# A fused vision block on one core: stages moved between steps, two sets of DMAs given to ScalarE's queue

## The chip, the cores and the metric

One core of a Trainium2 chip runs one launch of the kernel. The metric is device time in microseconds (us). Engines are named as in the profile: PE is TensorE (PEld its weight loads), DVE is VectorE, ACT is ScalarE, POOL is GpSimd, SP is the sync engine, which here only starts DMAs.

## The reference

Input x is 128 images of 12 x 224 x 224 in float32, 308 MB. Three stages follow each other; LN is a layer norm over the last axis.

```python
pooled = x.reshape(B, 12, 14, 16, 14, 16).sum(axis=(3, 5))        # 16x16 patch sums
h = einsum('bcij,ce->bije', pooled, channel_weights)              # (128, 196, 192)
y = LN(h); q = y[:, :64]; k = v = y[:, 64:]
a = softmax(einsum('bqc,bkc->bqk', q, k) / 4) @ v                 # 64 queries, 132 keys
a = transpose(a, (0, 2, 1)).reshape(B, 64, 192) @ proj_w.T + proj_b
h = h + concatenate([a, k], axis=1)
z = LN(h); scores = sigmoid(z @ gate_weight.T)                    # 8 experts
w, idx = best 2 of 8, limited to the best 2 of 4 pairs
out = h + sum over the 2 experts of w * ((silu(z@w1.T) * (z@w3.T)) @ w2.T) + the same for a shared expert
```

## The kernel before

**Groups and steps.** The images go in 8 groups of 16. The expert layers of a group are 63 steps: 7 chunks of rows times 9 experts (8 routed, the ninth shared). Chunks 0 to 4 (steps 0 to 44) are the key tokens, 384 to 512 rows each, whose first layer is one bf16 matmul per half (L1524). Chunks 5 and 6 (steps 45 to 62) are the queries, whose first layer is five fp32r matmuls per half (L1353). A step on each engine:

- PE, step s: first half of layer 1 for step s+1, second half for step s, layer 2 of step s-2 (L1509), then the items that a plan puts at step s. Before the first of these it waits for the silu of step s-1, whose PSUM bank it overwrites.
- ACT, step s: the silu of step s+1 (L913), at steps 1, 10, 19, ... an eviction of the chunk's output (L890), then its items, then its part of a tile of x (L801, one instruction per patch column).
- POOL, step s: multiplies silu by the gate weight row (L752), then items.
- DVE, step s: h = product of both halves (L1266), items, its part of a tile (L960).
- SP: one DMA per routed step that spreads one gate weight row over 128 partitions (L561, 5 steps ahead), the loads of x (1.8 MB a tile, 3 slots, L506), the stores, the stacking copies.

ACT loads a function table whenever it changes between silu and exp.

**Items.** While group g is in its expert layers, two plans bring the next data along. AK_PLAN (steps 39 on, group g+1): tok and V (patch sums transposed), stats and pow (variances, power on POOL), Xw and X (key rows in bf16 pieces), Uw and U, 28 gate operations of DVE (gate_k, L1177 to L1226), CK (gate weights to DRAM by ACT's queue). AQ_PLAN (steps 0 to 38, group g): PHT and VHT (transposed heads; VHw is their DVE part), S (scores), exp (L822), sum, ET (transposed probabilities, L1416), AH (times values, L1421), M (projection, L1426, copied to Msb by ACT L856), then H (L1449 and L1450: the residual rows, 8 rounds), stat_q, x2, XT (L1458), GQ, G, gate_q, CQ (L1482). Between M and H four DMAs (L532) of each half stack Msb into Mst; H waits for their semaphore `mixed`. MIX says that SP issues them at steps 11 and 17.

**Tiles.** 21 tiles of x per group: EARLY gives steps 1 to 34 to ten of them (three parts each, in three steps running), LATE steps 40 to 61 to eleven (two parts). A part costs DVE one reduce and ACT 1 to 3 columns. POOL takes two columns of each of the first 31 tiles (pool_tile, L663 and L658).

**Head.** Before group 0 there are no expert layers: 21 tiles are summed as they land, then steps 39 to 62 of the plans run alone for group 0, together with eleven tiles of group 1. Then the first silu starts. The groups 1 to 4 run in a hardware loop of two groups per turn.

## Time and profile before

| | us |
|---|---|
| median of 3 runs | 1794.09 |
| lowest and highest | 1784.72, 1795.03 |
| profiled execution, its own time | 1794.41 |
| its span in the profile | 1792.6 |
| head, until the first h | 198 |
| one group | 197 to 207 |
| PE busy | 1509.6 |
| DVE busy | 1178.3 |
| ACT busy | 879.1 |

Busy time is the sum of an engine's instructions; DMA-issuing instructions are not in it, although they hold the queue of the engine that issues them. In timeline rows the number in brackets is how long the engine had been idle before the row, with what released it.

### The profile page before, as it was taken

How to read it: one execution, taken by the hardware profiler on the slowest of the kernel's cores; microseconds unless marked ns; L12 is line 12 of the kernel's file. 1: busy time of each engine (PE TensorE's matmuls, PEld its weight loads, DVE VectorE, ACT ScalarE, POOL GpSimd, SP SyncE). 2: the span in 40 equal slices, each digit the busy share in tenths (PEclk: the TensorE clock that was granted, in tenths of full speed). 3: DMA queues.
4: the chain of work that ended last, by engine and by line, in shares of the span. 5: the costliest groups of instructions: out<-in, count | busy, mean ns of one | idle time of the engine just before them, and what ended most of it. 6: DMA issues, size and time to landing. Idle time of an engine off the chain costs nothing. (4 is left out here: it accounts for less than half of the span.)

```text
span 1792.6 us, 29976 instructions
## 1 busy us (share of the span) xinstructions
PE 1509.6 (84%) x9094; PEld 1184.0 (66%) x9094; DVE 1178.3 (66%) x2060; ACT 879.1 (49%) x2809; POOL 761.5 (42%) x761
## 2 busy tenths in 40 slices
PE   1721698999899988989899988999899988999997
PEld 1201575877668765877668765777668765887686
DVE  5856686687768666667768676677768666355511
ACT  2333655556545645547535655546545644335310
POOL 4327244633373234623464243633373233733431
PEclk9955799999999989999999999999999989999998
DMA  9897777778677777777777687768777775223320
GB/s 341 358 361 276 300 276 272 276 276 291 245 280 260 281 262 268 273 275 274 256 247 297 241 292 278 276 253 299 256 263 280 268 262 158 70 64 111 96 84 24
DMA packets 127672, 440.11 MB, mean 246 GB/s; under 512 B 14221, under 2 KB 80930, under 8 KB 105998
## 3 DMA queue, kind: packets, MB, share of 16 engines
q1 hardware_dynamic: 126390, 436.79, 67.6%
q10 hardware_dynamic: 1112, 1.30, 0.3%
q8 instruction: 76, 1.25, 0.3%
q14 instruction: 94, 0.77, 0.1%
...
## 5 line engine op out<-in xcount | busy, mean ns | idle before, releaser
L752 POOL TENSOR_TENSOR ffn<-ffn 128x384 f32<-128x384 f32 (+2 forms) x448 | 510.3, 1144 | 888.7 <-ACT ffn L913 810.2
L1509 PE MATMUL bank<-W2T,ffn 128*128 128x192 f32 (+1 forms) x3600 | 705.7, 333 | 10.2 <-ACT stage L890 5.0
L1509 PEld LDWEIGHTS bank<-W2T,ffn 128*128 128x128 f32 (+1 forms) x3600 | 604.9, 191 | 79.8 <-issue 16.5
L1266 DVE TENSOR_TENSOR ffn<-bank,ffn 128x384 f32<-128x384 f32 (+2 forms) x504 | 310.4, 617 | 349.3 <-PE bank L1353 151.8
L960 DVE TENSOR_REDUCE pooled<-xt 128x3 f32<-128x768 f32 (+2 forms) x375 | 447.8, 1195 | 18.5 <-DMA xt<-in_x 17.9
L913 ACT ACTIVATE ffn<-bank 128x384 f32<-128x384 f32 (+2 forms) x504 | 272.3, 542 | 370.3 <-PE bank L1524 141.3
L801 ACT ACTIVATE xt<-xt 128x256 f32<-128x256 f32 x809 | 329.7, 414 | 83.7 <-DMA xt<-in_x 76.1
L1524 PE MATMUL bank<-X2T,Wx 126*128 126x384 bf16 (+2 forms) x720 | 202.6, 355 | 46.7 <-DVE ffn L1266 31.9
L801 ACT ACTIVATION_READ_ACCUMULATOR xt<-xt 128x1 f32 x809 | 158.6, 196 | 0.0
L1353 PE MATMUL bank<-x0h,WT0h 128*128 128x512 f32 x288 | 130.5, 453 | 6.0 <-DVE ffn L1266 6.0
L1524 PEld LDWEIGHTS bank<-X2T,Wx 126*128 126x128 bf16 x720 | 58.2, 100 | 103.7 <-DVE ffn L1266 46.1
L1353 PE MATMUL bank<-x1l,WT1s 128*128 128x512 f32 x288 | 113.9, 395 | 0.0
L1353 PE MATMUL bank<-x1h,WT1s 128*128 128x512 f32 x288 | 113.8, 395 | 0.0
L1353 PE MATMUL bank<-x0l,WT0h 128*128 128x512 f32 x288 | 113.6, 395 | 0.0
L1353 PE MATMUL bank<-x0h,WT0l 128*128 128x512 f32 x288 | 113.6, 394 | 0.0
L707 POOL TENSOR_TENSOR stat<-stat,mhalf 98x16 f32<-98x16 f32 x32 | 94.8, 2970 | 21.9 <-DVE stat L1085 13.6
L1353 PEld LDWEIGHTS bank<-x0h,WT0h 128*128 128x128 f32 x288 | 54.3, 189 | 24.6 <-DVE ffn L1266 9.0
L1353 PEld LDWEIGHTS bank<-x1l,WT1s 128*128 128x128 f32 x288 | 54.0, 188 | 13.1
L1353 PEld LDWEIGHTS bank<-x0l,WT0h 128*128 128x128 f32 x288 | 54.0, 188 | 13.0
L1353 PEld LDWEIGHTS bank<-x1h,WT1s 128*128 128x128 f32 x288 | 54.0, 188 | 13.0
L1353 PEld LDWEIGHTS bank<-x0h,WT0l 128*128 128x128 f32 x288 | 54.4, 189 | 5.9
L841 ACT CAST UTq<-bank 126x128 bf16<-126x128 f32 x64 | 17.0, 265 | 84.0 <-PE bank L1433 84.0
...
## 6 DMA issues: line engine op xcount, KB each, us to landing
...
ffn<-cw_rows SPq DMA_DIRECT2D x192, 256.0 KB, 6.8
ffn<-cw_rows SPq DMA_DIRECT2D x192, 192.0 KB, 8.8
out<-stage SPq DMA_DIRECT2D x192, 96.0 KB
...
```

Of the source, the lines that this page charges most:

```text
L707: nc.gpsimd.tensor_tensor(out=stat[:, 3 * a + 1, u], in0=stat[:, 3 * a, u], in1=mhalf[0:HT, u], op=ALU.pow).then_inc(rstd_ready, 1)
L752: nc.gpsimd.tensor_tensor(out=cwb[slot][:, 0:n], in0=silu[(g.par + step) % 2][:, 0:n], in1=cwb[slot][:, 0:n], op=ALU.mult).then_inc(scaled, 1)
L801: last = nc.scalar.activation(src[:, :, j, :], src[:, :, j, :], ACT.Copy, accum_out=pooled[:, t // HALF, at:at + 1])
L841: nc.scalar.copy(UTq[:, :].rearrange("p (b t) -> p b t", b=GB)[:, 2 * i:2 * i + 2, :], src[:, :, 0:NQ])
L913: nc.scalar.activation(silu[(g.par + step) % 2][:, 0:n], h_ps(g, step, 0)[:, 0:n], ACT.Silu)\
L960: ins = v.tensor_reduce(out=pooled[:, t // HALF, at + lo:at + hi], in_=src[:, lo:hi, :, :], axis=AX.XY, op=ALU.add)
L1266: v.tensor_tensor(out=h[step % HR][:, 0:n], in0=h_ps(g, step, 1)[:, 0:n], in1=(silu[p] if e == NE else cwb[(c * NE + e) % CW_RING])[:, 0:n ...
L1353: ins = mm(o, left[q], right[q], start=(q == 0), stop=(q == len(left) - 1))
L1509: last = mm(o, h[step % HR][:, 128 * t:128 * t + m], W2T[:, e, :], start=(e == 0 and t % 2 == 0), stop=(e == NE), skip_group_check=True)
L1524: last = mm(o[:, 0:n], Wx[:, w:w + INTER], X2T[:, col:col + n], start=True, stop=True)
```

## The change

1. AQ_PLAN and AK_PLAN get other steps. PHT, VHT 0 and both VHw move from the group's start to the end of the group before (59 to 62); exp goes from steps 5 and 11 to 3 and 10, ET, S, M and H one step or so; gate_q is spread over steps 31 to 38 (3 or 4 a step) in place of 30 to 35 (5 a step); CQ goes from 36 to 39; the AK plan starts one step later and ends its gates two steps sooner, CK moves from 59 to 57, X takes three rounds a step.
2. EARLY becomes every third step from 1 to 28, LATE moves by a step or two.
3. The stacking copies ("mix") and the first five weight rows of a group ("row") are issued by ACT, at steps 11 and 18, and 60 and 61.
4. At every third step of a chunk (s % 9 == 2) PE does its items before layer 2.
5. In the head, POOL sums only group 0's tiles, and a table of its own (FIRST) says at which step DVE and ACT sum group 1's eleven.

```diff
 AQ_PLAN = {
...
-    5: [("U", 7), ("exp", 0)],
-    6: [("ET", 0), ("sum", 0)],
+    3: [("exp", 0), ("U", 7)],
+    4: [("sum", 0)],
+    5: [("ET", 0)],
...
-    11: [("exp", 1)],
+    10: [("exp", 1), ("M", 1)],
+    11: [("sum", 1), ("mix", 0)],
...
+    18: [("stat_q", 0), ("mix", 1)],
...
-MIX = {11: 0, 17: 1}
-A_FIRST = 39
+A_FIRST = 40
...
-    AQ_PLAN.setdefault(30 + _n // 5, []).append(("gate_q", _n))
-    AK_PLAN.setdefault(53 + _n // 5, []).append(("gate_k", _n))
+    AQ_PLAN.setdefault(31 + _n * 8 // GATES, []).append(("gate_q", _n))
+    AK_PLAN.setdefault(51 + _n // 5, []).append(("gate_k", _n))
...
-LATE = {s: i for i, s in enumerate([40, 44, 46, 48, 50, 52, 53, 55, 57, 59, 61])}
-EARLY = {s: len(LATE) + i for i, s in enumerate([1, 5, 8, 12, 16, 20, 23, 27, 31, 34])}
+LATE = {s: i for i, s in enumerate([41, 44, 46, 47, 49, 50, 52, 54, 56, 58, 60])}
+EARLY = {s: len(LATE) + i for i, s in enumerate([1, 4, 7, 10, 13, 16, 19, 22, 25, 28])}
+FIRST = {41: 0, 42: 1, 43: 2, 44: 3, 46: 4, 47: 5, 50: 6, 57: 7, 58: 8, 59: 9, 60: 10}
-POOL_TILES = TILES + len(LATE) - 1
+POOL_TILES = TILES
...
+                if kind == "mix":
+                    act.wait_ge(aux_act, g.at(BYACT[-1], BYACT[R[("M", 2 * i + 1)]]))
+                    for m in range(4):
+                        act.dma_start(Mst[:, 4 * i + m, :],
+                                      Msb[2 * CH * m:2 * CH * (m + 1), i, :]).then_inc(mixed[i], 16)
+                    return
+                if kind == "row":
...
+                    act.dma_start(cwb[i][:, 0:n], cw_rows[g.par, i, 1024:1024 + n].partition_broadcast(128))\
+                       .then_inc(cw_landed[i], 16)
...
                     layer1(g, step, 1)
+                    if step % EX == 2:
+                        step_pe(g, step, left)
                     if step >= 2:
                         layer2(g, step - 2)
...
-                    step_pe(g, step, left)
+                    if step % EX != 2:
+                        step_pe(g, step, left)
```

ACT's order around steps 10 to 13 of a group in the loop, before. L890 is the eviction, L856 the copy of M, L913 a silu, L822 the exp, L851 the copy of ET, L801 tile columns.

```order
L890 COPY stage<-bank 128x384 [waits out_stored1]
L890 COPY stage<-bank 128x192
L828 REGISTER_ALU
L856 COPY Msb<-bank 96x192 [waits aux_full]
L801 ACTIVATE xt,pooled<-xt 128x16x16 [waits x_in1]
...
L913 ACTIVATE ffn<-bank 128x384 [waits scaled]
L821 REGISTER_ALU
L822 ACT_TABLE_LOAD
L822 ACTIVATE attw<-attw 64x8x132 [waits aux_dve]
...
L913 ACT_TABLE_LOAD
L913 ACTIVATE ffn<-bank 128x384 [waits scaled]
```

The same place in the changed kernel, whose lines are 9 or 10 further on: L899 is the eviction, L812 the exp, L865 the copy of M, L791 tile columns, L922 a silu, L818 the stacking DMAs.

```order
L899 COPY stage<-bank 128x192
L811 REGISTER_ALU
L812 ACT_TABLE_LOAD
L812 ACTIVATE attw<-attw 64x8x132 [waits aux_dve]
...
L865 COPY Msb<-bank 96x192 [waits aux_full]
L791 ACTIVATE xt,pooled<-xt 128x16x16 [waits x_in2]
...
L922 ACT_TABLE_LOAD
L922 ACTIVATE ffn<-bank 128x384 [waits scaled]
...
L818 DMA h2q<-Msb 72x1x192 [waits aux_act]
L818 DMA h2q<-Msb 72x1x192 x3
...
L922 ACTIVATE ffn<-bank 128x384 [waits scaled]
```

Eviction and exp now stand between the same two silus, and the four DMAs stand ahead of the next one.

PE's order at step 20, before: the first H of the second half comes behind layer 2 (L1509).

```order
L1524 MATMUL bank<-X2T,Wx 128x512 [waits silu_done]
L1524 MATMUL bank<-X2T,Wx 128x512 [waits h_done]
L1493 REGISTER_ALU
L1509 MATMUL bank<-W2T,ffn 128x192 [waits evac_act]
...
L1449 MATMUL bank<-CWx,UTq 128x192 [waits mixed_second,aux_dve]
L1450 MATMUL bank<-h2q,CWr 128x192
```

In the changed kernel, where L1533 is layer 1, L1458 and L1459 are H, and L1518 is layer 2:

```order
L1533 MATMUL bank<-X2T,Wx 128x512 [waits silu_done]
L1533 MATMUL bank<-X2T,Wx 128x512 [waits h_done]
L267 REGISTER_ALU
L1458 MATMUL bank<-CWx,UTq 128x192 [waits mixed_second,aux_act]
L1459 MATMUL bank<-h2q,CWr 128x192
L1502 REGISTER_ALU
L1518 MATMUL bank<-W2T,ffn 128x192 [waits evac_act]
```

H, with its wait for the stacking DMAs, now stands ahead of layer 2.

## Rows read from the trace of the kernel before

**Rows 1.** The page: busy time, share of the span and instructions of each engine.

```profile
PE 1509.6 (84%) x9094; PEld 1184.0 (66%) x9094; DVE 1178.3 (66%) x2060; ACT 879.1 (49%) x2809; POOL 761.5 (42%) x761
```

**Rows 2.** Windows: head, group 1, last group. Length, then busy time of each engine.

```profile
0.00:198.00 198.00, 66.26 (x254) 31.82 (x254) 129.57 (x179) 69.03 (x303) 90.18 (x187) 0.73 0.86 328
396.60:595.00 198.40, 180.09 (x1118) 143.44 (x1118) 143.83 (x251) 110.28 (x359) 86.56 (x75) 0.99 0.76 275
1603.00:1792.00 189.00, 170.37 (x1036) 138.16 (x1034) 72.98 (x156) 58.62 (x113) 64.16 (x57) 0.98 0.27 79
```

**Rows 3.** Timeline of PE in group 1, rows that followed idle time.

```profile
397.88 0.68 PE L1402 MATMUL bank<-ident,attw 64*128 64x64 f32 x8 [1.87 <-DVE attw L1105]
411.70 0.62 PE L1416 MATMUL bank<-ident,attw 64*98 64x64 f32 x8 [1.84 <-issue]
428.34 0.62 PE L1416 MATMUL bank<-ident,attw 64*98 64x64 f32 x8 [0.92 <-issue]
437.74 0.26 PE L1449 MATMUL bank<-CWx,UTq 126*128 126x192 bf16 x1 [1.19 <-DMA h2q<-Msb]
451.56 0.63 PE L1458 MATMUL bank<-ident,attw 128*128 128x128 f32 x4 [1.09 <-DVE attw L1146]
480.35 0.50 PE L1524 MATMUL bank<-X2T,Wx 126*128 126x384 bf16 x2 [0.96 <-ACT ffn L913]
485.74 0.34 PE L1524 MATMUL bank<-X2T,Wx 126*128 126x384 bf16 x1 [2.08 <-DVE ffn L1266]
491.39 0.36 PE L1524 MATMUL bank<-X2T,Wx 126*128 126x448 bf16 x1 [0.83 <-DVE ffn L1266]
494.54 1.03 PE L1482 MATMUL bank<-ident,gt 128*8 128x128 f32 x8 [1.81 <-DVE gt L1226]
517.40 0.50 PE L1353 MATMUL bank<-x0h,WT0h 128*128 128x512 f32 x1 [0.78 <-DVE ffn L1266]
563.96 1.57 PE L1509 MATMUL bank<-W2T,ffn 128*128 128x192 f32 x8 [0.72 <-DVE stage L1247]
```

**Rows 4.** POOL's timeline: the first scaling of group 2 and the wait before it.

```profile
593.20 0.99 POOL L752 TENSOR_TENSOR ffn<-ffn 128x384 f32<-128x384 f32 x1 [8.86 <-DMA ffn<-cw_rows]
```

**Rows 5.** Window of DVE over the gate_q steps of group 1.

```profile
480.00:497.00 17.00, 14.82 (x36) 0.90 0.80 284
```

**Rows 6.** ACT's timeline, group 1, steps 10 to 12: eviction, M copy, table load, exp, tile column.

```profile
423.62 0.70 ACT L890 COPY stage<-bank 128x384 f32<-128x384 f32 x2 [0.17 <-PE bank L1509]
424.75 0.31 ACT L856 COPY Msb<-bank 96x192 f32<-96x192 f32 x1 [0.43 <-PE bank L1426]
...
425.86 1.28 ACT L822 ACT_TABLE_LOAD   x1
427.16 1.08 ACT L822 ACTIVATE attw<-attw 64x1056 f32<-64x1056 f32 x1
...
430.40 0.43 ACT L801 ACTIVATE xt<-xt 128x256 f32<-128x256 f32 x1
```

**Rows 7.** Windows over all engines from that eviction to step 14; one step with H.

```profile
423.62:430.88 7.26, 6.34 (x50) 5.06 (x49) 4.93 (x7) 6.77 (x14) 2.75 (x3) 1.00 1.01 408
442.32:444.17 1.85, 1.85 (x13) 1.57 (x12) 1.85 (x5) 1.25 (x5) 1.54 (x2) 1.00 0.87 340
```

**Rows 8.** DMA issues: four stacking copies on SP (timeline); setup copies on ACT (ns min/median/max).

```profile
426.64 3.40 SPq L532 DMA_DIRECT2D h2q<-Msb  x4
L816 ACTq DMA_DIRECT2D Wx<-ffn x6: 726/736/1339, 89.0 to 93.5; - x6
```

**Rows 9.** Group 2: PE's timeline at the first H, and the window after it.

```profile
638.16 0.34 PE L1449 MATMUL bank<-CWx,UTq 126*128 126x192 bf16 x1 [4.06 <-DMA h2q<-Msb]
640.00:650.00 10.00, 10.00 (x41) 7.72 (x40) 5.23 (x12) 4.22 (x15) 2.58 (x3) 0.65 0.57 199
```

**Rows 10.** Timeline of the head: POOL, DVE and ACT.

```profile
136.91 0.73 POOL L663 TENSOR_TENSOR ffn<-xt 128x256 f32<-128x256 f32 x1
138.86 2.91 POOL L707 TENSOR_TENSOR stat<-stat,mhalf 98x16 f32<-98x16 f32 x1
...
169.20 2.27 DVE L960 TENSOR_REDUCE pooled<-xt 128x8 f32<-128x2048 f32 x1
...
187.14 0.34 ACTq L872 DMA_DIRECT2D cw_rows<-attw  x1
...
195.84 0.87 ACT L913 ACTIVATE ffn<-bank 128x384 f32<-128x384 f32 x2
```

More of the change, by code:

```diff
@@ L107 @@
     27: [("XT", 3)],
[L108 to L113 removed]
+    29: [("GQ", 0), ("GQ", 1)],
+    30: [("G", 0)],
+    39: [("CQ", 0), ("CQ", 1)],
+}
+A_FIRST = 40
 AK_PLAN = {
[L115 to L135 removed]
+    40: [("fin", 0), ("tok", 0), ("V", 0)],
+    41: [("stats", 0), ("pow", 0)],
+    42: [("pow", 1)],
+    43: [("stats2", 0), ("pow", 2)],
+    44: [("pow", 3)],
+    45: [("Xw", 0)],
+    46: [("Xw", 1), ("Xw", 2)],
+    47: [("Xw", 3)],
+    48: [("X", 0), ("X", 1), ("X", 2)],
+    49: [("X", 3), ("X", 4), ("X", 5), ("Uw", 0)],
+    50: [("keyG", 0), ("keyG", 1), ("GK", 0), ("Uw", 1)],
+    51: [("Uw", 2)],
+    52: [("Uw", 3)],
+    53: [("U", 0)],
+    54: [("U", 1)],
+    55: [("U", 2)],
+    56: [("U", 3)],
+    57: [("CK", 0), ("CK", 1), ("CK", 2)],
+    58: [("CK", 3), ("CK", 4)],
+    59: [("PHT", 0)],
+    60: [("PHT", 1), ("VHw", 0), ("row", 0), ("row", 1), ("row", 2)],
+    61: [("VHT", 0), ("row", 3), ("row", 4)],
+    62: [("VHw", 1)],
 }
@@ L191, in tiles_at @@
         found.append((g.plus(1), EARLY[step]))
-    if left >= 2 and step in LATE:
-        found.append((g.plus(2), LATE[step]))
+    late = FIRST if g.k is None and g.off < 0 else LATE
+    if left >= 2 and step in late:
+        found.append((g.plus(2), late[step]))
     return found
@@ L550, in cw_load @@
                 back = use - CW_RING
-                if use == 0:
+                if use == CW_AHEAD:
                     sp.wait_ge(cw_out[0], g.at(16, 16))
@@ L564, in step_dma @@
             def step_dma(g, step, left):
-                if step >= 61 and left:
-                    for ahead in ((0, 1) if step == 61 else (2, 3, 4)):
-                        cw_load(g.plus(1), ahead)
-                elif step + CW_AHEAD < STEPS and g.off >= 0:
+                if step + CW_AHEAD < STEPS and g.off >= 0:
                     cw_load(g, step + CW_AHEAD)
@@ L588, in ffn_dma @@
                         store(g.minus(1), NCH - 1)
-                    if step in MIX:
-                        stack_mix(g, MIX[step])
             for t in range(TILES):
@@ L822, in item @@
                     nc.scalar.activation(E[:, :, NQ:TOK], E[:, :, NQ:TOK], ACT.Exp).then_inc(exp_done, 1)
+                    return
[4 more added lines that the diff above has]
+                                      Msb[2 * CH * m:2 * CH * (m + 1), i, :]).then_inc(mixed[i], 16)
+                    return
+                if kind == "row":
+                    if i == 0:
+                        act.wait_ge(cw_out[0], g.at(16, 16))
+                    back = i + CW_USES - CW_RING
+                    wait(act, h_done, g.minus(1).at(STEPS, back // NE * EX + back % NE + 1) if g.k is not None or g.off else 0)
+                    if i == CW_RING - 1 or g.k is None and g.off == 0:
+                        act.wait_ge(rows_used, POOL_TILES)
+                    n = CHUNKS[0][2]
+                    act.dma_start(cwb[i][:, 0:n], cw_rows[g.par, i, 1024:1024 + n].partition_broadcast(128))\
+                       .then_inc(cw_landed[i], 16)
                     return
```

58 lines of the change are left out of this document (13 added, 45 removed).

## The prediction

> **What bounds the kernel now.** I read the page's busy times first, then windows by group, then PE's timeline for the rows that follow idle time, then the engine each of them names. The page [rows 1] gives PE 84% of the span, DVE 66%, ACT 49% and POOL 42%: the bound is PE, but not at every place. The windows [rows 2] say where it isn't. In the head PE works 66.3 of 198 us. In group 1 it works 180.1 of 198.4 us, so 18.3 us of a group are idle, and in the last group 18.6 of 189.0. No other engine is near full in group 1 (DVE 143.8, ACT 110.3, POOL 86.6), so the 18.3 us are waits at single places, and only those can be won. PE's timeline [rows 3] has most of them: 1.87 at the group's start, 1.84 before ET of the first half, 0.92 before ET of the second, 1.19 at the first H, 1.09 at XT, 0.96 + 2.08 + 0.83 + 1.81 = 5.68 in the gate zone, 0.78 and 0.72 late in the group, together 14.1. A change that moves items can win those and can open new ones, since the items are a chain and the silus stand in the same ACT queue.
>
> **The change part by part.** All terms are for group 1 and taken for groups 0 to 6; the head and the last group follow. PE's arithmetic is the same in both kernels.
>
> Start of a group. PE waits 1.87 for VHT [rows 3], because POOL's scaling stood for 8.86 us until its first weight rows had landed [rows 4], behind x loads on SP's queue. Now ACT issues these rows at steps 60 and 61 and VHT is made a step before the border. The wait goes, and what is late next (the silu of step 1) has a step of PE work as cover: -1.9.
>
> ET of the first half. Two steps between exp and ET where there was one. The exp itself is two table loads of 1.28 and 1.08 of work [rows 6], which still stand between two silus, so the 1.84 shrinks to some 1.2: -0.6.
>
> Steps 10 to 14. This is the costliest edit. Before, the eviction stood at step 10 and the exp at 11. Now both stand between the silus of steps 11 and 12, with M's copy and two tile columns: 0.70 + 1.28 + 1.08 + 0.31 + 2 x 0.43, a load back 1.28 and the silu 0.44 (half of 0.87, [rows 10]) = 5.95 [rows 6]. PE can't start step 13 before that silu. Then come the four DMAs. Six setup copies on ACT's queue took a median of 736 ns each [rows 8], so 2.9 us; SP's four took 3.4. With two columns and the next silu that is 2.9 + 0.86 + 0.44 = 4.2 more, 10.2 in all. PE has 6.34 us of work in that window [rows 7], and 0.65 of it (scores, moved to step 9) is gone: 5.7. So 4.5 us of stall, 2.1 before step 13 and 2.4 before step 14, in place of 0.92 + 1.19 = 2.11 [rows 3] of which the second comes again as follows. H waits for the copies' landing. On SP the issue ended at 430.04 [rows 8] and H began at 437.74 [rows 3], 7.7 us later; I take 4.5 on ACT's queue, an estimate between that and nothing, which makes H some 1.9 late after the steps between. The bounds: from 0 (if the issue returns early, or falls where ACT waits for PE) to 5.1 (if landing takes 7.7 again). Sum 4.5 + 1.9 - 2.11, plus 0.4 for the shorter lead at ET: +4.7, bounds -2 to +8.
>
> Second half, steps 18 to 20. The DMAs are issued at 18, a step later than before, and H at 20 stands ahead of layer 2. From M on PE: copy 0.31, columns 0.86, silu 0.44, issue 2.9, landing 4.5 less what the first of four gains, about 3: 7.5. PE has two steps of 1.85 [rows 7] and an H round of 0.5, some 4.2, in that time: 3.3 of stall. XT's 1.09 [rows 3] behind it is absorbed: +2.2, bounds -1.1 (all covered) to +5.5.
>
> Gate zone. DVE is busy 14.82 of 17.00 us there [rows 5], so each wait of PE for h is a wait for a full DVE. Tile parts leave steps 31 to 38 (EARLY ends at 28) and the gates fall from five a step to three or four. The waits for DVE, 2.08 + 0.83 + 1.81 [rows 3], fall to about 1; the 0.96 behind ACT stays: -3.7, with bounds 0 and -5.7. The tile parts pushed forward meet a DVE that is busy 4.93 of 7.26 and 1.85 of 1.85 us [rows 7], so some of this comes back; I take 0.1.
>
> Late steps. 0.78 and 0.72 [rows 3] fall to 0.6 together by PE's order at every third step of a chunk and by CK two steps sooner, and X with three rounds a step on two PSUM banks costs 0.6: -0.3, bounds -1.5 to +1.
>
> A group: -1.9 - 0.6 + 4.7 + 2.2 - 3.6 - 0.3 = +0.5, and of that 0.2 is taken off because part of ACT's stall hides PE's waits for h in the same steps: +0.3, seven groups +2.
>
> Head. POOL's sum stood ahead of pow: 136.91 to 138.86 [rows 10], 2.0 us, and three such leave the chain that ends the head: -6. Behind it DVE did tile sums of 2.27 [rows 10] between gates, three of them in the chain: -6.8. But not all of the 12.8 is won, since ACT's tail is now the longer: CK's copies and DMAs from 187.14 [rows 10], tiles of four or five columns at 0.43 [rows 6], five rows at 0.74 [rows 8], the copies for PHT and a table load before the silu at 195.84 [rows 10]. By these some 3 us are won, and 1.7 us of group 0's first PE work is done in the head: -4.7. Bounds: 0 (ACT eats all) and -12.8. The head's loads of x (DMA share 0.86, [rows 2]) don't change.
>
> Last group. No tiles and no next group: 4.7 and 2.2 without the columns' shares (3.9 and 1.5), start and ET -2.5, gates -1: +2.
>
> Clock. After a wait of 4.06 us at an H in group 2, the granted clock over the next 10 us was 0.65 of full [rows 9], partly the lower level of 1.2 GHz instead of 2.4. Stalls of 2 and more at steps 13, 14 and 20 could bring that; shorter waits in the gate zone could save some. I set 0, bounds -12 (1.7 a group saved) and +28 (3.5 a group: at 0.65 ten microseconds hold 6.5 of work).
>
> The sum: 1794.4 of the profiled execution (span 1792.6 and 1.8 around it) + 2 - 4.7 + 2 = 1793.7. That execution lay 0.3 above the median of 1794.1, so the forecast is 1793.4, rounded to 1793.5: the kernel gives back at steps 10 to 20 what it wins elsewhere.
>
> **Rivals.**
>
> R1, the issue on ACT costs PE nothing (faster). ACT has 88 us idle in group 1 [rows 2] and in parts of this zone waits for PE; if exp and DMAs fall into those, or if the four copies land soon after issue, then the +4.7 and +2.2 shrink to 0 or below. Seven a group over 7.5 groups is 52: 1741; with half of it 1767. For it speaks the 7.7 us that SP's copies took to land in one place [rows 8] and the 4.06 wait in the next group [rows 9]: SP's queue is the one with the x loads, and a queue of its own may have them land in 2. Against it speaks ACT's 6.77 busy of 7.26 us in just this window [rows 7], before anything was added. The Trainium skill bears on this: DMA: Bandwidth & Descriptors, Queues, rings and completion order, says that each DMA engine takes turns between the queue rows it has work for, packet by packet, and SP and ACT have a row each. By this rule ACT's copies don't wait behind a whole x load and R1's landing holds. No run here yet shows it.
>
> R2, slower: the stall before H starves PE long enough for the clock. Its place is steps 13 to 15 and 20. If landing on ACT's queue takes the 7.7 us of SP's [rows 3, 8], H is 3.2 later; if after it the clock does what [rows 9] show, 3.5 go with it. One of both in each group is 3.4 x 8 = 27: 1820; both are 54: 1847. It decides from a granted clock under 0.9 behind step 14 in most groups. For it: PE in this zone goes from 6.34 of 7.26 us to 5.7 of 10.2. Against: the gaps are short single ones, of 2 to 3 us, where the one shown was 4.06. The Trainium skill's own page, Trainium Kernel Development and Optimization, Key Constraints, says that queues of SP, ACT and POOL run on the same 16 DMA engines and that issuing from several saves only the issuer's time. By that, landing stays at 7.7 and this rival is the nearer one; the DMA share of 1.01 in [rows 7] agrees that the engines are full there.
>
> R3, the change doesn't do what it says. LATE now puts x tiles at steps 46 and 47 and at 49 and 50, one step apart, with three slots; a load can start only when the slot's last sum is done. If the second of each pair waits for its load, DVE and with it h is 1 to 3 us late twice a group, which takes back the gate zone's gain: 1794 + 7.5 x 3 = 1816 at worst.
>
> **How the numbers follow.** A measurement of this kernel can tell about 1% (18 us) from no change. The forecast, gains and losses within 18 us of each other: 0.42. R1, 0.34, centred on 1760 with a tail to 1735. R2 and R3 together 0.24 (0.18 and 0.06), centred on 1825. Range: below 1745 lies a quarter of R1, 0.08; above 1830 two fifths of the slower cases, 0.1. So 1745 to 1830; the likeliest case's own range is 1776 to 1812. Chances: faster by over 1% 0.34, within 1% 0.42, slower by over 1% 0.24.
>
> **What would show it.** POOL's wait at a group's start and PE's at VHT gone. ACT's timeline: the four DMAs of about 0.74 each between two silus, and PE idle 2 us before each of steps 13 and 14: if that idle is under 1, R1 is right. The first H's releaser: DMA with more than 2 us of idle is my forecast or R2, and a landing under 2 us after the issue is R1. PE's waits for h in the gate zone under 1.5 us together. The clock in the windows behind step 14 under 0.9: R2. First silu of the head near 193; if it is before 188, ACT's tail was costed too high. PE's idle in group 1 near 18.6 of about 198.7 us. A group under 194 or over 201 us would make the forecast wrong.

## The result, and the profile after

The changed kernel takes 1887.97 us (median of 4 runs, 1882.68 to 1891.90), the kernel before 1794.56 in the runs beside it: the ratio is 1.053, with a 95% interval of 1.047 to 1.058. The forecast was 1793.5 with a range to 1830. The change costs 93 us, and the forecast was wrong in sign and outside its range.

The page of the changed kernel, engine busy times, as in [rows 1]:

```profile
PE 1568.7 (83%) x9094; PEld 1233.2 (65%) x9094; DVE 1185.5 (63%) x2060; ACT 884.7 (47%) x2829; POOL 745.2 (39%) x721
```

PE executes the same 9094 matmuls and is busy 59.1 us longer. The span grew by 97.5 (1890.1 for 1792.6), so 59 of them are matmuls that ran at a lower clock, and 38 are idle time.

Windows of the changed kernel over the head, group 1 and the last group, columns as in [rows 2]; a group is cut at the end of its first h:

```profile
0.00:194.20 194.20, 70.73 (x278) 35.16 (x278) 132.50 (x183) 74.39 (x327) 71.82 (x146) 0.71 0.87 335
402.00:614.50 212.50, 187.26 (x1119) 149.89 (x1118) 143.80 (x251) 110.76 (x358) 86.99 (x75) 0.94 0.72 256
1697.90:1889.50 191.60, 170.72 (x1021) 138.28 (x1019) 72.36 (x153) 56.75 (x110) 64.08 (x57) 0.97 0.28 78
```

Group 1 is 212.5 long instead of 198.4: PE's busy time rose by 7.2 and its idle time from 18.3 to 25.2, while DVE, ACT and POOL work the same time as before. The granted clock over the group is 0.94 for 0.99.

Where in the group? Windows of PE by stage in group 1 of the kernel before, cut where DVE ends the h of a step. Shown are steps 15 to 17, 18 to 22, 31 to 40 and 48 to 50. After the PE busy time stand granted clock, DMA share and GB/s.

```profile
...
433.52:442.67 9.15, 7.96 (x53) 1.00 1.04 353
442.67:455.98 13.31, 12.01 (x72) 1.00 0.84 294
...
478.38:505.67 27.29, 20.21 (x103) 0.94 0.84 289
...
528.45:539.78 11.33, 11.31 (x65) 1.00 0.95 368
...
```

The same four stages in the changed kernel:

```profile
...
441.88:458.89 17.01, 10.82 (x71) 0.80 0.76 276
458.89:476.87 17.98, 14.07 (x69) 0.81 0.68 250
...
498.35:518.69 20.34, 17.46 (x106) 1.00 0.70 242
...
545.00:563.51 18.51, 13.70 (x76) 0.82 0.60 220
...
```

Steps 15 to 22 went from 22.5 to 35.0, and 48 to 50 from 11.3 to 18.5, each with a clock of 0.80 to 0.82 where it had been full. The gate zone fell from 27.3 to 20.3. With a whole group cut into four zones in the same way, the mean length over groups 0 to 6 is, before and after: steps 0 to 11, 30.7 and 33.2; 12 to 22, 31.4 and 44.0; 23 to 47, 72.7 and 67.6; 48 to the next 0, 65.9 and 70.0. So +2.6 + 12.6 - 5.1 + 4.0 = +14.1 a group, 99 for seven. The head is 3.8 shorter, the last group 2.5 longer, which makes the 97.5.

PE's timeline in group 1 of the changed kernel, rows after idle time, to be read against [rows 3] (L1458 is H, L1416 S, L1452 X, L1491 CQ):

```profile
407.78 0.30 PE L1416 MATMUL bank<-PHT,VHT 128*64 128x34 f32 x2 [1.05 <-DVE attw L1125]
409.90 0.43 PE L1442 MATMUL bank<-identb,SPT 98*126 98x98 bf16 x4 [0.70 <-DVE attw L1125]
417.29 0.50 PE L1533 MATMUL bank<-X2T,Wx 126*128 126x384 bf16 x2 [1.21 <-ACT ffn L922]
436.73 0.50 PE L1533 MATMUL bank<-X2T,Wx 126*128 126x384 bf16 x2 [2.14 <-ACT ffn L922]
448.06 0.34 PE L1458 MATMUL bank<-CWx,UTq 126*128 126x192 bf16 x1 [6.28 <-DMA h2q<-Msb]
466.81 0.32 PE L1458 MATMUL bank<-CWx,UTq 126*128 126x192 bf16 x1 [3.91 <-DMA h2q<-Msb]
...
506.06 0.34 PE L1533 MATMUL bank<-X2T,Wx 126*128 126x384 bf16 x1 [0.71 <-DVE ffn L1275]
508.40 0.36 PE L1533 MATMUL bank<-X2T,Wx 126*128 126x448 bf16 x1 [0.83 <-DVE ffn L1275]
516.62 1.03 PE L1491 MATMUL bank<-ident,gt 128*8 128x128 f32 x8 [0.90 <-DVE gt L1235]
...
551.06 2.17 PE L1452 MATMUL bank<-identb,SPT 98*126 98x34 bf16 x16 [4.51 <-DVE SPT L1073]
```

Three waits carry most of the idle time that was added: 6.28 before the first H (7.12 to 8.88 in groups 2 to 6), 3.91 before the fifth (1.5 in four of the six groups 1 to 6), and 4.51 before X, where before had none. The waits of the gate zone, 5.7 in sum before, are 0.71 + 0.83 + 0.90 now.

**What an idle PE costs afterwards.** Windows of PE in group 2, around the wait of 7.12 that ended at 661.3:

```profile
650.00:654.00 4.00, 3.34 (x24) 1.00 0.98 375
...
658.00:662.00 4.00, 0.71 (x3) 0.50 1.02 393
662.00:666.00 4.00, 4.00 (x21) 0.50 0.85 321
666.00:670.00 4.00, 4.00 (x29) 0.50 0.12 40
670.00:674.00 4.00, 4.00 (x12) 0.50 0.53 170
```

The clock is at its lower level of 1.2 GHz (0.50) before the wait ends, and stays there for 12 us of full work behind it. Steps 15 to 17 on PE, from the first matmul of one step's layer 1 to that of another, took 8.4 us before (the median of groups 1 to 5) and take 15.7 (10.2 and 10.4 in groups 1 and 4, 15.8 or 15.9 in 2, 3 and 5). At X it is the same on a smaller scale: 0.50 from 551 to 555, then 0.68.

In group 1 the clock had fallen already before the first H, behind the 2.14 us for ACT's silu:

```profile
437.00:441.00 4.00, 4.00 (x22) 0.64 0.99 370
```

Summed over the profile, the time at the lower clock in the four zones was 1.5, 3.4, 3.4 and 0.7 us a group before, and is 5.2, 18.5, 0 and 7.2 in the changed kernel.

### The profile page after: what moved, and what is told of

Same layout as the page of the kernel before. It is cut to its first block and busy times, and to the rows that moved or that the text cites. A ratio compares the mean times of both kernels' runs of the same rounds, so it can differ in the third digit from the quotient of the medians.

```text
span 1890.1 us, 29906 instructions
## 1 busy us (share of the span) xinstructions
PE 1568.7 (83%) x9094; PEld 1233.2 (65%) x9094; DVE 1185.5 (63%) x2060; ACT 884.7 (47%) x2829; POOL 745.2 (39%) x721
## 5 line engine op out<-in xcount | busy, mean ns | idle before, releaser
L742 POOL TENSOR_TENSOR ffn<-ffn 128x384 f32<-128x384 f32 (+2 forms) x448 | 512.0, 1147 | 1009.1 <-ACT ffn L922 964.8
L1518 PE MATMUL bank<-W2T,ffn 128*128 128x192 f32 (+1 forms) x3600 | 725.1, 340 | 3.6 <-DVE stage L1256 1.9
L1518 PEld LDWEIGHTS bank<-W2T,ffn 128*128 128x128 f32 (+1 forms) x3600 | 625.5, 197 | 71.0 <-issue 19.8
L969 DVE TENSOR_REDUCE pooled<-xt 128x3 f32<-128x768 f32 (+3 forms) x385 | 450.5, 1175 | 28.4 <-DMA xt<-in_x 27.3
L922 ACT ACTIVATE ffn<-bank 128x384 f32<-128x384 f32 (+2 forms) x504 | 270.9, 541 | 390.8 <-PE bank L1533 186.2
L791 ACT ACTIVATE xt<-xt 128x256 f32<-128x256 f32 x819 | 333.8, 414 | 117.0 <-DMA xt<-in_x 79.2
L1533 PE MATMUL bank<-X2T,Wx 126*128 126x384 bf16 (+2 forms) x720 | 206.1, 363 | 39.6 <-ACT ffn L922 22.7
L791 ACT ACTIVATION_READ_ACCUMULATOR xt<-xt 128x1 f32 x819 | 159.6, 195 | 0.0
L1533 PEld LDWEIGHTS bank<-X2T,Wx 126*128 126x128 bf16 x720 | 63.2, 102 | 91.3 <-issue 28.5
L697 POOL TENSOR_TENSOR stat<-stat,mhalf 98x16 f32<-98x16 f32 x32 | 94.7, 2960 | 23.3 <-DVE stat L1094 13.5
L1458 PE MATMUL bank<-CWx,UTq 126*128 126x192 bf16 x64 | 17.5, 274 | 68.8 <-DMA h2q<-Msb 68.8
L1452 PE MATMUL bank<-identb,SPT 98*126 98x34 bf16 (+1 forms) x256 | 27.5, 255 | 56.7 <-DVE SPT L1073 54.0
L1139 DVE BATCH_NORM_STATS2 bst<-bank 128x6 f32<-128x192 f32 x64 | 23.1, 361 | 71.9 <-PE bank L1459 71.6
L1362 PEld LDWEIGHTS bank<-x0h,WT0h 128*128 128x128 f32 x288 | 56.5, 196 | 15.8 <-issue 7.5
```

The lines of the kernel that those rows point to most:

```text
L697: nc.gpsimd.tensor_tensor(out=stat[:, 3 * a + 1, u], in0=stat[:, 3 * a, u], in1=mhalf[0:HT, u], op=ALU.pow).then_inc(rstd_ready, 1)
L742: nc.gpsimd.tensor_tensor(out=cwb[slot][:, 0:n], in0=silu[(g.par + step) % 2][:, 0:n], in1=cwb[slot][:, 0:n], op=ALU.mult).then_inc(scaled, 1)
L791: last = nc.scalar.activation(src[:, :, j, :], src[:, :, j, :], ACT.Copy, accum_out=pooled[:, t // HALF, at:at + 1])
L922: nc.scalar.activation(silu[(g.par + step) % 2][:, 0:n], h_ps(g, step, 0)[:, 0:n], ACT.Silu)\
L969: ins = v.tensor_reduce(out=pooled[:, t // HALF, at + lo:at + hi], in_=src[:, lo:hi, :, :], axis=AX.XY, op=ALU.add)
L1139: v.bn_stats(bst[:, i, 0:6], ps[:, 0:D])
```

## Why the copies landed so late

The queues in steps 10 to 13 of group 1, changed kernel. SP first, L508 the x loads, L556 the weight rows:

```profile
425.38 3.90 SPq L556 DMA_DIRECT2D ffn<-cw_rows  x2
429.60 0.34 SPq L508 DMA_DIRECT2D xt<-in_x  x1
430.05 1.59 SPq L556 DMA_DIRECT2D ffn<-cw_rows  x3
431.95 0.34 SPq L508 DMA_DIRECT2D xt<-in_x  x1
```

ACT's rows in the same stretch, L818 the stacking copies:

```profile
431.50 1.28 ACT L812 ACT_TABLE_LOAD   x1
432.79 1.08 ACT L812 ACTIVATE attw<-attw 64x1056 f32<-64x1056 f32 x1
...
434.10 0.85 ACTq L818 DMA_DIRECT2D h2q<-Msb  x1
...
434.89 1.28 ACT L922 ACT_TABLE_LOAD   x1
434.99 1.60 ACTq L818 DMA_DIRECT2D h2q<-Msb  x2
436.18 0.49 ACT L922 ACTIVATE ffn<-bank 128x384 f32<-128x384 f32 x1
436.61 0.78 ACTq L818 DMA_DIRECT2D h2q<-Msb  x1
437.44 0.42 ACT L791 ACTIVATE xt<-xt 128x256 f32<-128x256 f32 x1 [0.77 <-issue]
```

Two things are seen. The DMAs hold ACT for less than I had costed: the table load and the silu, which stand ahead of them in ACT's program, run while they are issued, and only what stands behind them waits, 0.77 us, until the last issue has ended at 437.39. And two x loads of 1.8 MB left SP 2.35 us apart just ahead of the copies. The load of step 7 was late, because SP stood on the stores of step 5 and on rows, so it met that of step 10. For the second of them, the source view of L508 says

```profile
DMA to landing us min/median/max: 13.4/13.4/13.4
```

so it landed at 445.4, and the copies at 448.0. The trace's landing records show the same in the other kernels: the copies land at about the time of the last x load that was issued ahead of them or among them. Group 1, all times in us; a group starts at the end of its first h:

```
kernel    group    last x load (*)       copies issued   landed  after   queue  PE
          starts   issued, landed                                issue          waits
before    396.6    426.2  436.3          426.6 - 430.0   437.7   7.7     SP     1.19
after     402.0    431.9  445.4          434.1 - 437.4   448.0   10.6    ACT    6.28
a_mixsp   399.5    428.1  444.2          431.8 - 435.2   446.0   10.8    SP     6.57
a_early   402.0    436.0  446.5          435.4 - 438.7   447.4   8.7     ACT    6.37
a_h15     398.2    429.1  442.6          431.7 - 435.0   445.2   10.2    ACT    1.26
b_early   399.1    427.3  441.7          429.2 - 432.6   443.6   11.0    SP     2.25
b_mixact  398.8    428.4  439.8          427.6 - 430.9   439.8   8.9     ACT    none
a_gap     403.3    430.9  441.6          436.8 - 440.1   444.7   4.7     ACT    1.90
a_small   399.9    429.5  432.3 (small)  433.6 - 436.9   438.3   1.4     ACT    none
b_small   395.1    426.1  429.2 (small)  426.6 - 430.0   431.5   1.4     SP     none

(*) issued ahead of the last of the four copies
```

With a load in flight the first copies of group 1 come in 0 to 3.2 us behind its landing (4.2 in b_best, where the load had landed 1.2 behind their issue), and in groups 2 to 6 from 0.5 ahead of it to 3.9 behind, on SP's queue and on ACT's alike. With small loads, which have landed before the last issue, they come 1.4 to 1.8 us after it. So the landing goes with the loads in flight and not with the queue. One difference between the queues is left: in the last group, where no x load is in flight, the second set landed 2.7 to 3.1 us after its last issue on ACT's queue and 1.4 or 1.5 on SP's, in every run; no run explains it. What inside the DMA engines ties a copy to a load isn't shown either.

## The experiments

Labels that begin with a_ are edits of the changed kernel, those with b_ of the kernel before. "Zones" are the four of the means above (0 to 11, 12 to 22, 23 to 47, 48 to the next 0). Ratios are to the kernel before as run beside each; its medians there were 1791.1 to 1798.2.

**Which cause holds the copies (a_early, a_mixsp, a_h15), and X (a_x49).**

```diff
-EARLY = ... [1, 4, 7, 10, 13, 16, 19, 22, 25, 28]
+EARLY = ... [1, 5, 8, 12, 16, 20, 23, 27, 31, 34]
```

> The changed kernel with EARLY as before (1, 5, 8, 12, 16, 20, 23, 27, 31, 34). In the changed kernel two x loads left SP at 429.60 and 431.95 and the four stacking copies (issued 434.10 to 437.39) landed 10.6 us after the last; PE waited 6.3 for them at step 14 and ran steps 15 to 17 at half clock. Theory A (the copies land when the x loads issued just ahead of them are through, and the changed kernel bunches two): with the loads further apart the landing falls to about 7.5 us, the wait by 3 and part of the half clock goes: 5 to 10 us a group, 1820 to 1850 in all, minus the gate zone, which loses up to 2 a group since tiles come back to steps 27 to 36. Theory B (the lead between issue and H is a step shorter) and theory C (ACT's queue lands later than SP's) say the landing stays near 10 and the time between 1880 and 1905.

Measured: 1883.06 (1862.55 to 1884.87), 1.044 of before (1.036 to 1.053). Zone 12 to 22 fell from 44.0 to 40.2, zone 23 to 47 rose from 67.6 to 70.6. The first is what theory A wanted, but too small: the load of step 11 now went out among the copies and kept them just as well. The second says that 3 of the 5.1 us won in steps 23 to 47 belong to the tiles that left the gate zone.

```diff
-    11: [("sum", 1), ("mix", 0)],
+    11: [("sum", 1)],
...
-    18: [("stat_q", 0), ("mix", 1)],
+    18: [("stat_q", 0)],
...
+MIX = {11: 0, 18: 1}
...
+            def stack_mix(g, half):
...
+                    if step in MIX:
+                        stack_mix(g, MIX[step])
```

> The changed kernel with the stacking copies back on SP, at steps 11 and 18. Theory C (ACT's queue lands later): landing falls from 10.6 to about 7.7 and the issue comes earlier, so 5 to 12 us a group: 1800 to 1850. Theory A (landing follows the x loads in flight, whatever the queue): the landing ends at the same moment, that of the x loads, so within 1% of 1888; only ACT's 3.2 us of issue between two silus go, which PE pays with 2.1 of idle before step 13 at most: 1870 to 1890.

Measured: 1867.28 (1863.08 to 1869.63), 1.039 (1.033 to 1.045). In group 1 the copies were issued at 431.78, which is 32.3 us after the group's start as against 32.1, so no sooner, and landed 10.8 after the last issue, 1.8 behind the x load (its landing took 16.1). Theory C falls: the queue doesn't set the landing. PE's two waits were 6.57 and 3.59:

```profile
446.05 0.34 PE L1468 MATMUL bank<-CWx,UTq 126*128 126x192 bf16 x1 [6.57 <-DMA h2q<-Msb]
464.37 0.32 PE L1468 MATMUL bank<-CWx,UTq 126*128 126x192 bf16 x1 [3.59 <-DMA h2q<-Msb]
```

PE's idle time before step 13 stayed at 2.14, so the DMAs on ACT's queue aren't its cause. The 20 us that it won are more than theory A gave; they stand in zone 12 to 22 (41.1) and in a last group 3.5 shorter, where the fifth H waits 1.23 us instead of 2.90. In zone 12 to 22 the lower clock ended sooner (steps 15 to 17 took 10.5 for 15.7); why isn't settled.

```diff
-    14: [("H", 0)],
-    15: [("AH", 1), ("H", 1)],
-    16: [("M", 2), ("H", 2)],
-    17: [("M", 3), ("H", 3)],
-    18: [("stat_q", 0), ("mix", 1)],
+    14: [("AH", 1)],
+    15: [("M", 2), ("H", 0)],
+    16: [("M", 3), ("H", 1)],
+    17: [("H", 2), ("mix", 1)],
+    18: [("H", 3)],
+    19: [("stat_q", 0)],
```

> The changed kernel with H, M of the second half and stat_q one step later, as before (H from 15 on), the second copies at step 17. Theory B (the lead is what is lost): H gets one more step, 1.9 us at full clock, so its wait falls from 7.3 to 5.4, still long enough for the half clock: 2 to 3 us a group, about 1870. If the half clock is what costs (7 us a group in steps 15 to 17) and it hangs on the length of the wait, it could fall to 1840. Theory A alone: the moment of landing doesn't move, so PE's wait moves behind more work and the gain is that of B, 2 a group, no more.

Measured: 1848.44 (1844.63 to 1848.99), 1.029 (1.023 to 1.035). The wait at the first H fell from 6.3 to 1.3 in group 1 and to 3.6 at most in groups 2 to 6, more than the step of 1.9 that I gave it. AH with its 1 us of work also came ahead of it; the other 2 us aren't explained. Behind a wait of 1.3 the clock stayed full:

```profile
445.00:449.00 4.00, 3.72 (x22) 1.00 0.96 376
449.00:453.00 4.00, 4.00 (x26) 1.00 1.11 436
453.00:457.00 4.00, 1.05 (x7) 1.00 0.97 333
457.00:461.00 4.00, 2.02 (x7) 0.53 1.07 412
461.00:465.00 4.00, 4.00 (x16) 0.62 0.55 217
```

The last three rows show the loss move: the second copies, issued at 448.6 behind the load of step 16, kept the fifth H for 4.9 us, and the clock fell there. Zone 12 to 22 is 37.5, half way back to 31.4, and the time at the lower clock in it 8.8 us a group for 18.5.

```diff
-    48: [("X", 0), ("X", 1), ("X", 2)],
-    49: [("X", 3), ("X", 4), ("X", 5), ("Uw", 0)],
+    49: [("X", 0), ("X", 1), ("X", 2)],
+    50: [("X", 3), ("X", 4), ("X", 5), ("Uw", 0)],
...
-    AK_PLAN.setdefault(51 + _n // 5, []).append(("gate_k", _n))
+    AK_PLAN.setdefault(52 + _n // 5, []).append(("gate_k", _n))
```

> The changed kernel with X, Uw, U, the key gates and CK one step later (X at 49 and 50). In the changed kernel PE waits 4.51 at step 48 for the copy of SPT, which ended at 551.0, and the next step is at half clock (5.69 instead of 3.63). Theory: X overtook POOL's and DVE's work for it; a step later the wait is gone and the half clock with it: 4.5 + 2.1 + 0.5 = 7 us for each of the seven groups, 1888 - 49 = 1839. Rival (POOL is late anyway, the wait moves to step 49): under 2 us a group, above 1875.

Measured: 1859.78 (1856.58 to 1870.84), 1.036 (1.029 to 1.044). PE still waited 2.14 at X in group 1 (2.10 to 2.26 in the others), and in six of the seven groups the clock stood at 0.50 for 3.4 us behind it; the last zone went from 70.0 to 66.9. Something of both: X had overtaken POOL, by more than a step.

**One part alone (a_gap, b_mixact, b_head, b_gates).**

```diff
-EARLY = ... [1, 4, 7, 10, 13, 16, 19, 22, 25, 28]
+EARLY = ... [1, 4, 9, 12, 15, 18, 21, 24, 27, 30]
```

> The changed kernel with EARLY at 1, 4, 9, 12, 15, ... 30: no tile at step 7, so no x load leaves SP at step 10, just ahead of the stacking copies of step 11. In the five kernels run so far the copies landed 0.9 to 2.6 us after the last x load that had been issued ahead of them, on either queue, and 1.4 us after their own issue where none was in flight. If this is the rule, the first half's copies (issue about 434) land with the load of step 7 (about 438 + 1.6), before PE needs them (441.7): the wait of 6.3 to 8.9 and the half clock after it (steps 15 to 17 back from 15.7 to about 9 us) go, 12 to 14 us a group for six groups: 1888 - 80 = 1808, plus up to 10 for tile parts back in steps 31 and 32. If the landing hangs on something else (the lead, the busy DMA engines as such), it stays 8 to 10 us after the issue and the time at 1870 or more.

Measured: 1858.38 (1855.65 to 1866.01), 1.035 (1.030 to 1.039). The copies followed the loads in both halves, and the second undid the gain of the first:

```profile
444.79 0.26 PE L1458 MATMUL bank<-CWx,UTq 126*128 126x192 bf16 x1 [1.90 <-DMA h2q<-Msb]
469.25 0.32 PE L1458 MATMUL bank<-CWx,UTq 126*128 126x192 bf16 x1 [6.62 <-DMA h2q<-Msb]
```

The first wait is gone (none to 1.9), but the load of step 18 now left at 460.7 between the second copies (459.4 to 462.6), and these landed at 469.1: 6.6 to 9.5 of wait in groups 1 to 6 for 1.5 to 4.1. I had only looked at the first copies.

b_mixact gives the four DMAs to ACT in the kernel before:

```diff
-    11: [("exp", 1)],
+    11: [("exp", 1), ("mix", 0)],
...
-    17: [("H", 2)],
+    17: [("H", 2), ("mix", 1)],
...
-MIX = {11: 0, 17: 1}
...
+                if kind == "mix":
...
+                        act.dma_start(Mst[:, 4 * i + m, :],
```

> The kernel before with its stacking copies on ACT's queue, at steps 11 and 17, nothing else. By the rule (landing follows the x loads in flight, not the queue) the landing moment stays, 1.4 us after the load of 426.2 has landed; ACT is held 3.3 us at step 11, behind the exp: within 1% of 1794, 0 to 1.5 us a group slower. If ACT's own queue were better, H's waits (1.2 to 4.1) would go: 1780. If the hold of ACT costs what the prediction said (2.4 a half): up to 1825.

Measured: 1806.11 (1802.32 to 1821.82), 1.008 (1.005 to 1.011): 10 us slower, 1.2 a group. This is the price of the queue by itself, a ninth of the loss. H's waits fell (1.1 at most in groups 1 to 6, for 1.2 to 4.1), although the copies landed 8.9 to 9.8 us after their last issue, no sooner than on SP's queue (7.4 to 10.5). Zone 12 to 22 is 31.7 for 31.4; 1.3 of the loss of a group stands in steps 23 to 47 (74.0 for 72.7), where there are no copies, and isn't explained.

b_head is FIRST and POOL_TILES in the kernel before:

```diff
-POOL_TILES = TILES + len(LATE) - 1
+POOL_TILES = TILES
+FIRST = {41: 0, 42: 1, 43: 2, 44: 3, 46: 4, 47: 5, 50: 6, 57: 7, 58: 8, 59: 9, 60: 10}
...
+    late = FIRST if g.k is None and g.off < 0 else LATE
```

> The kernel before with the head of the change alone: POOL sums only group 0's tiles, and FIRST. In the changed kernel the first h came 3.8 us sooner (193.7 for 197.5). Expected: the same 3 to 5 us, 1790, so within 1%, with the first h at 193 to 195. Rival: the rest of the head's gain came from the plans, and FIRST alone gives under 1 us.

Measured: 1792.99 (1783.88 to 1802.60), 0.998 (0.996 to 1.001). The first h ended at 195.0 instead of 198.1, 3.1 us sooner; the whole time can't be told from the kernel before's.

b_gates spreads gate_q alone:

```diff
-    36: [("CQ", 0), ("CQ", 1)],
+    39: [("CQ", 0), ("CQ", 1)],
...
-    AQ_PLAN.setdefault(30 + _n // 5, []).append(("gate_q", _n))
+    AQ_PLAN.setdefault(31 + _n * 8 // GATES, []).append(("gate_q", _n))
```

> The kernel before with gate_q spread over steps 31 to 38 and CQ at 39, tiles where they were. In the changed kernel steps 31 to 40 took 22.6 us instead of 27.7 a group; with the old tile places (a_early) 25.8. So the spread alone should give 1.9 a group, the other 3.2 needing the tiles out of the zone: 1794 - 15 = 1779, perhaps a little more since PE doesn't change order here. If the gates' spread gives nothing without the tiles: 1794.

Measured: 1793.87 (1786.50 to 1801.71), 0.9995 (0.997 to 1.002). The spread gives nothing while the tiles are there: zone 23 to 47 is 73.1 for 72.7. The expectation of 15 us was wrong.

**The cause taken away, and the repairs together (a_small, a_order, a_fix, b_best).**

a_small loads only one eighth of each row of x from group 2 on, while all other work stays:

```diff
-                sp.dma_start(xt[:, slot, :], x_rows(g.num(), t)).then_inc(x_in[slot], 16)
+                n = ROW if g.k is None and g.off <= 1 else ROW // 8
+                sp.dma_start(xt[:, slot, 0:n], x_rows(g.num(), t)[:, 0:n]).then_inc(x_in[slot], 16)
```

> The changed kernel with the x loads of groups 2 to 7 cut to an eighth of each row (what is summed after that is left-over data). If x loads in flight are what keeps the copies from landing, they land about 1.5 us after the issue from group 1 on, PE's 6.3 to 8.9 of step 14 go, the half clock of steps 15 to 17 with it, and the 1.5 to 3.9 at step 20 stay for the part that is ACT's issue: 12 to 14 us a group for groups 1 to 5: 1888 - 65 = 1823 or less, as other waits for DMA go too; the 4.5 at step 48 stays, being POOL's. If the copies are slow by themselves (ACT's queue, their shape, the writes), their landing stays near 10 us and the time over 1860.

Measured: 1803.35 (1798.20 to 1808.32), 1.004 (1.002 to 1.006) of the full kernel before: 85 us less than the changed kernel. The copies landed 1.4 or 1.5 us after their last issue, no first H waited from group 1 on, and the 1.5 at the fifth H stayed. Zone 12 to 22 was 32.9 instead of 44.0, though all plans were those of the change.

a_order puts PE's items behind layer 2 again at every step:

```diff
-                    if step % EX == 2:
-                        step_pe(g, step, left)
...
-                    if step % EX != 2:
-                        step_pe(g, step, left)
+                    step_pe(g, step, left)
```

> The changed kernel with PE's items behind layer 2 at every step. The prediction put 3.3 of stall on H standing ahead of layer 2 at step 20; there PE waits 1.5 to 3.9. With layer 2 (1.1 us) ahead the wait falls by 1.1 and PE isn't idle meanwhile: 1 us a group, about 1880. It could also lose as much elsewhere (step 11's and 38's items), then 1888. No theory expects more than 1%.

Measured: 1887.24 (1883.61 to 1894.83), the changed kernel's own time within its runs. The fifth H no longer waits (0.6 us at most in groups 1 to 6), the first still waits 5.3 to 8.2, and the whole time doesn't tell the two orders apart.

a_fix puts three repairs together: H and the copies of a_h15, X of a_x49, and

```diff
-EARLY = ... [1, 4, 7, 10, 13, 16, 19, 22, 25, 28]
+EARLY = ... [1, 4, 9, 12, 17, 20, 23, 26, 29, 32]
```

> The changed kernel with three moves at once: no x load issued just ahead of either set of copies (EARLY 1, 4, 9, 12, 17, 20, ... 32), H, M of the second half and the second copies as before (H from 15, copies at 17), X and what follows one step later. If the loss is these three places, the groups fall by 6 (steps 12 to 14), 6.8 (15 to 17) and 2.9 (48 to 62), with steps 18 to 22 unchanged at 15: 15.7 for six groups and a half, 1888 - 102 = 1786, as fast as before or a little faster. If something else of the change costs, it stays above 1810.

Measured: 1814.53 (1803.86 to 1822.12), 1.010 (1.007 to 1.014): 73 of the 93 us are back, 28 less than I added up. Zone 12 to 22 is 33.2, but at the fifth H 2.8 to 4.3 remain in groups 1 to 6 (the copies at step 17 still come behind the load of step 15), X still waits 2.1, and the gate zone gave back 2.2, since tiles reach to step 34 again.

b_best is the kernel before with what had won:

```diff
-    36: [("CQ", 0), ("CQ", 1)],
+    38: [("CQ", 0), ("CQ", 1)],
...
-    AQ_PLAN.setdefault(30 + _n // 5, []).append(("gate_q", _n))
+    AQ_PLAN.setdefault(30 + _n * 8 // GATES, []).append(("gate_q", _n))
...
-EARLY = ... [1, 5, 8, 12, 16, 20, 23, 27, 31, 34]
+EARLY = ... [1, 4, 9, 12, 16, 19, 22, 25, 28, 31]
```

and FIRST and POOL_TILES as in b_head.

> The kernel before with what won in the changed one: tiles out of the gate zone (EARLY 1, 4, 9, 12, 16, 19, ... 31, which also keeps x loads from going out just ahead of the first copies), gate_q in eight steps 30 to 37, CQ at 38, and the head with FIRST. Gate zone 27.7 to about 23.5, H's wait of 1.2 to 4.1 gone, head 2: 5.5 a group and 2, 1795 - 40 = 1755. If the second copies at step 17 now meet the load of step 15, 3 to 6 us a group come back: 1780.

Measured: 1771.41 (1767.78 to 1775.55), 0.986 (0.982 to 0.991): faster than both kernels. In group 1 no first H waits, the fifth waits 2.55:

```profile
446.02 0.24 PE L1451 MATMUL bank<-CWx,UTq 126*128 126x192 bf16 x1 [2.55 <-DMA h2q<-Msb]
```

Zone 12 to 22 is 29.2 for 31.4, zone 23 to 47 71.0 for 72.7, the first h at 193.4. The gate zone won less than half of what I expected.

**What was still open (b_small, b_early, a_x39).** b_small makes the edit of a_small in the kernel before.

> The kernel before with the x loads of groups 2 to 7 cut to an eighth of each row. H's waits of 1.2 to 4.1 for the copies go, as does part of the wait for weight rows at a group's start (1.9): 3 to 4 us a group for six groups, 1797 - 22 = 1775. Then the changed kernel with the same loads (1803) is 28 slower, 4 a group, and of its 90 us of loss about 62 are x loads in flight. If before gains nothing (1795), then 82 of the 90 are.

Measured: 1766.82 (1763.78 to 1772.59), 0.986 (0.982 to 0.991). So with small loads the change still costs 36.5 us (1803.35 - 1766.82; 32 by the two ratios, since the two ran at different times), and 57 to 61 of its 93 exist only with the full x loads. The four zones of the pair, b_small first and then a_small, are 32.3 and 31.5, 28.2 and 32.9, 73.0 and 67.5, 62.8 and 69.4. So with the late landing away the change costs 4.7 a group in steps 12 to 22, where ACT's stall before step 13 and the wait at the fifth H stay, and 6.6 from step 48 on, where X waits, and it wins 5.5 in steps 23 to 47.

b_early sets the change's EARLY in the kernel before, and nothing else.

> The kernel before with the change's EARLY alone (1, 4, 7, ... 28). By the rule the copies (issued at 427) land 1.5 us after the load of step 10, which goes out just ahead of them behind that of step 7: at 439 to 441 instead of 437.7, so H at step 15 waits 2 to 4 us more in each group, perhaps with half clock; tiles out of the gate zone give 3 back. So 1785 to 1810, no clear change. If EARLY alone is the culprit it is 1830 or more.

Measured: 1803.21 (1799.47 to 1804.90), 1.005 (1.002 to 1.008). The copies of group 1 landed 44.5 us after its start for 41.1, the first H waited 1.1 to 2.4 in most groups and the fifth 0.8 to 5.8; zone 23 to 47 fell by 2.9, to 69.8. The new EARLY is a small loss where H has its old lead, and a large one where it hasn't.

a_x39 gives the changed kernel the chain before X of the kernel before (fin at 39, powers to 43, Xw one a step to 48, X at 49).

> The changed kernel with the chain of the next group's rows as before: fin and tok at step 39, powers to 43, Xw one a step from 45 to 48, X at 49 and 50. If the wait of 4.5 at step 48 came from a chain started a step later with X a step sooner, it goes as a whole: 48 to 62 from 70.1 to about 62 us a group, 8 x 7 = 56: 1832, against 1860 for X moved alone. If PE's wait for DVE's copy stays at step 49, 1860.

Measured: 1866.92 (1866.08 to 1869.12), 1.042 (1.038 to 1.046). The wait for DVE's copy at X is gone, and steps 48 to the next 0 are back at 65.7 (before: 65.9, changed: 70.0). The sum won is 21 and not 56: the last zone gives 4.3 a group and not 8, zone 23 to 47 grew by 0.8, since PE now waits 1.90 for h before the first layer of step 45 and 0.9 + 0.4 + 0.3 at step 39, where CQ meets fin, and the head grew by 3.7.

The chain itself, POOL in the changed kernel ahead of X at step 48 (L697 powers, L688 to L683 splitting, L742 scalings):

```profile
537.30 2.90 POOL L697 TENSOR_TENSOR stat<-stat,mhalf 98x16 f32<-98x16 f32 x1
...
544.08 0.83 POOL L676 TENSOR_TENSOR SPT<-val,ones 98x384 bf16<-98x384 f32 x1
...
546.88 0.90 POOL L683 TENSOR_TENSOR SPT<-res,SPT 98x384 bf16<-98x384 f32 x1
```

and DVE, whose copy X waits for:

```profile
547.82 3.19 DVE L1073 COPY SPT<-SPT 98x1344 bf16<-98x1344 bf16 x2 [2.81 <-POOL SPT L683]
```

In the kernel before that copy ended at 535.7, and X began at 535.77: the chain had no slack at all in groups 1 to 4, and 1.2 us in groups 0, 5 and 6, though no row of idle time showed it.

```profile
532.61 3.11 DVE L1064 COPY SPT<-SPT 98x1344 bf16<-98x1344 bf16 x2 [0.93 <-POOL SPT L693]
```

## Why the prediction was wrong, step by step

**The landing of the copies** is the step that failed most. The prediction took 4.5 us after the last issue, "an estimate between that and nothing", with 7.7 as the far bound. It was 10.6 in group 1 and 9.9 to 11.6 in groups 2 to 6. The 7.7 went with an x load that had left 0.5 us ahead of the copies and landed 1.4 us before them; I should have asked of [rows 8] what else was in flight, and where the new EARLY puts the loads at steps 7 and 10. The change's EARLY was costed for DVE's work and not for its loads.

**H's lead.** H moved from step 15 to 14 while AH went behind it and the issue came 2 us later in the group (32.1 us after its start for 30.1). I used this only to place the 1.9 of H's wait. a_h15 shows what it is worth: with one step more of lead the kernel takes 40 us less, the first H waits 5.0 less in group 1, and the time at the lower clock in steps 12 to 22 is halved.

**The clock** was set to 0 with a bound of +28. It cost 59 us of PE's busy time. R2 named the place, the granted clock under 0.9 behind step 14, and the two halves of its price; both came, each larger (a landing of 10.6 for 7.7, and 12 us and more at 0.50 for 10 at 0.65). Its full case gave 1847, the measurement 1888. So its mechanism was right, its size too small and its chance of 0.18 too low; the loss at X, 4.0 a group, wasn't in it.

**ACT's hold.** The stall before step 13 was forecast at 2.1 and is 2.14 (PE's row at 436.73 above). The sum 5.95 of eviction, exp and table loads is right (5.89 from 430.78 to the silu's end at 436.67), and a_mixsp, which has the same stall, shows that the DMAs have no part in it. The 2.4 before step 14 for the four DMAs didn't come: most of their issue ran beside the table load and the silu ahead of them, and the next silu ended 2.05 us after that one and not 4.2. b_mixact puts the whole price of ACT's queue at 10 us.

**Second half.** A stall of 3.3 was forecast at the fifth H. It is 3.91 and 4.08 in groups 1 and 4, and 1.5 in the other four of 1 to 6.

**X** was the other failed step: forecast at +0.6, it waited 4.5 in each group, with the lower clock behind it; the last zone grew by 4.0 a group, and X's own stage of group 1 by 7.2, of which 2.4 is PE's busy time. I had counted two PSUM banks and not POOL: the chain of powers and splits starts a step later in the change and is used a step sooner, and the row before it shows the work for it with no slack. None of the rivals had it.

**Gate zone.** Forecast -3.6; steps 23 to 47 fell by 5.1, the sign right and the reason in part. The tiles alone give 2.9 (b_early), and with the tiles back 2.1 stay (a_early). The spread of gate_q alone gives nothing (b_gates), so what holds these 2.1 wasn't separated; the clock, at 0.50 for 3.4 us a group in this zone before and not at all now, is part of it.

**Group start and ET.** The wait of 1.87 went, as forecast, and that of 1.84, forecast to shrink to 1.2, went whole, but 1.05 + 0.70 + 1.21 came for them, PE work moved in, and the clock was at 0.50 for 5.2 us a group instead of 1.5; steps 0 to 11 are 2.6 longer and not 2.5 shorter. With small loads they are no longer (31.5 in a_small, 32.3 in b_small).

**Head.** The ends of the gates chain moved as forecast:

```profile
174.87 0.33 ACTq L881 DMA_DIRECT2D cw_rows<-attw  x1
...
190.70 1.28 ACT L922 ACT_TABLE_LOAD   x1
192.00 0.87 ACT L922 ACTIVATE ffn<-bank 128x384 f32<-128x384 f32 x2
```

CK's first DMA came 12.3 us sooner than in [rows 10] (forecast 12.8), the first silu 3.8 sooner (forecast 3): ACT's tail took the rest, as the prediction said.

**R1** fell: the copies on a queue of their own landed no sooner. The rule of the Trainium skill that I set behind it (DMA: Bandwidth & Descriptors, Queues, rings and completion order: each DMA engine takes turns between the rows it has work for, packet by packet) gave no early landing here: 10.6 us after the last issue on ACT's queue, 10.8 on SP's in a_mixsp. The Trainium skill's other rule (Trainium Kernel Development and Optimization, Key Constraints: another issuing engine saves only issue time) is the one that the traces agree with: the landing is the same, and b_mixact won nothing. **R3** didn't come: no wait of PE at steps 46 to 50 goes back to a tile of x, and the one at 48 is POOL's chain.
